# Layer 0 state space: B products of every third unit by ScalarE and TensorE, two thirds of the C products on GpSimd

## The chip, the cores and the metric

The kernel runs on one core of a Trainium2 chip. The metric is the device time in microseconds (us) of that core, the median of three runs. A core has TensorE (PE, with its weight load PEld), VectorE (DVE), ScalarE (ACT), GpSimd (POOL) and the queue of SyncE (SP), which issues most DMAs. Each engine takes its own instructions in order and waits for the others at semaphores. PSUM is written by TensorE and can be read and written by VectorE and ScalarE here; GpSimd's operands all lie in SBUF.

## The reference

The model has two layers, each a state-space block and a mixture of experts. The change is in the state space of layer 0, on 4 batches of 1024 tokens with 256 inner channels and 16 states. Cut to what matters:

```
x_dbl = xp @ Wx.T                       # 64 + 16 + 16 columns
dlt, B, C = split(x_dbl)
delta = softplus(dlt @ Wdt.T + bdt)
A = -exp(A_log)
# for each channel d and each state n, over the tokens t:
h[t] = exp(delta[t,d] * A[d,n]) * h[t-1] + delta[t,d] * xp[t,d] * B[t,n]
y[t,d] = sum_n C[t,n] * h[t] + xp[t,d] * Dp[d]
out = (y * silu(z)) @ Wo.T
```

The reference works in chunks of 16 tokens; the kernel computes the same recurrence by one scan along the tokens.

## The kernel before

Channels lie on the 128 partitions in two halves (j = 0, 1), tokens along the free axis. A **unit** g is one state n of one column half c (512 tokens) of one batch b: a batch has UNITS = 32 units, TOTAL is 128. Position s is g % 32; s 0 to 15 are column half 0, s 16 to 31 half 1. `u` is delta times xp. For each unit

- ScalarE makes the decay exp(delta A) for both halves, `state_decay` (L563), into one of DS = 5 PSUM banks `decay`. Its wait is for the scan or C product five half-units back. In column half 0 it first copies the last column of the bank's former content to `carry` (L560), for the units whose states end in that bank.
- GpSimd makes the B product `bu` = u times row B, broadcast to all partitions, both halves in one instruction of 128x1024 (`make_bu`, L687), LEAD = 3 units ahead of its step. The row comes by a DMA of 256 KB (`load_b`, L222) into one of BS = 4 buffers; `bu` has BUS = 5 buffers.
- VectorE scans each half: state = decay * state + bu (L780), in place in the bank, or, in the units `on_pool` (s % 3 == 2), into the SBUF buffer `h` (HS = 6 buffers).
- The C product, state times row C (`load_c`, L231, CS = 5 buffers), is made by VectorE for each half (L790), and for the units on_pool by GpSimd in one instruction in place in `h` (`times_c`, L697), after a copy of the last column to `carry` (L695) in column half 0.
- TensorE adds h to `y_ps` by an identity matmul of 512 columns for each half (`add_state`, L416), two instructions each in the trace, for unit s - 2 at its step s.

The order on each engine is written out by hand. Every engine runs the same loop over b and s: at step g GpSimd makes B of g + 3, then C of g - 1 where that unit is its own; ScalarE makes the decays of g + 1. Between them stands the next batch's preparation, `pieces(b, s)`: x (four projections of 4 taps each, L336), z, low, v (L381, L386), each one made by TensorE in the single bank `piece` and read by ScalarE one step later, which frees it. ScalarE also has two silus of 1024 columns twice, each pair with two loads of its tables (s 12 for z, s 14 for x), softplus at s 23 to 25 and, from batch 1 on, the normalised rows `hat` from s 25. `gate` (L796) on VectorE takes y_ps of a column half at s 18 (half 0) and at s 1 of the next batch (half 1). TensorE's `skip` (L406) starts the next half of y_ps after it, `project_out` (L433) makes the output rows at s 22 and s 2. VectorE's `make_delta` is L801. After the stage come routing, experts, a second state space and its experts; the change doesn't touch them.

## Time and profile before

| | us |
|---|---|
| median of 3 runs | 1180.13 (1178.96 to 1181.77) |
| span of the profiled execution | 1175.1 |
| stage of layer 0's state space in it, first scan to the gate after the last | 35.6 to 505.0 |

The time of the profiled execution as a whole isn't given apart from its span. The median of the runs lies 5.0 us above the span, which is what lies around the span; sums are made in the span and these 5.0 us are added. Times in the rows are from the span's start. A busy time overlaps a little with the next instruction's, so an engine's pace is its start to start.

### The profile page before, as it was taken

To read this page: it belongs to the slowest core of one execution; us is meant where nothing else is said; L and a number is where in the kernel's file an instruction comes from. 1 tells how busy PE (TensorE), PEld (TensorE's weight loads), DVE (VectorE), ACT (ScalarE), POOL (GpSimd) and SP (SyncE) were. 2 spreads that over 40 slices of the span, in tenths; PEclk is the share of its full clock that TensorE was granted. 3 is DMA by queue.
4 is the path that set the end of the run, shared out by engine and by line. 5 is a ranking of instruction groups with operands and counts; after the bars stand their busy time and mean duration, and the time that the engine had idled before them with its cause. 6 is when DMAs were issued, how large, how long until landed. Compare 5 with 4: busy or idle time off the path is not lost. (4 is left out here: it accounts for less than half of the span.)

```text
span 1175.1 us, 14982 instructions
## 1 busy us (share of the span) xinstructions
PE 878.0 (75%) x4244; PEld 565.5 (48%) x4244; DVE 887.3 (76%) x1790; ACT 630.2 (54%) x1401; POOL 738.3 (63%) x508
## 2 busy tenths in 40 slices
PE   7797769886987787753999736596987978349930
PEld 4243324334433433333999713264665767339920
DVE  4896999899979999966666555486896878465512
ACT  4787635874587465516343313656567684246710
POOL 0898799989988999702666376355433443037646
PEclk8999989998999898865999967598989977569975
DMA  6644445455544554340233312111101020142323
GB/s 185 184 131 131 125 147 166 137 157 160 162 131 143 164 164 156 113 164 13 71 85 87 72 50 68 45 34 50 45 2 64 28 74 19 54 165 73 71 63 98
DMA packets 90905, 118.95 MB, mean 101 GB/s; under 512 B 12508, under 2 KB 48804, under 8 KB 90696
## 3 DMA queue, kind: packets, MB, share of 16 engines
q1 hardware_dynamic: 84168, 104.34, 28.7%
q0 software_dynamic: 6656, 13.64, 5.0%
q8 instruction: 36, 0.59, 0.2%
q14 instruction: 45, 0.37, 0.1%
HBM read 103.70 MB, written 14.25 MB: 100 GB/s over the span
## 5 line engine op out<-in xcount | busy, mean ns | idle before, releaser
L687 POOL TENSOR_TENSOR ma_bu<-ma_u,ma_row_b 128x1024 f32<-128x1024 f32 x128 | 300.7, 2377 | 15.6 <-DVE ma_u L898 8.0
L416 PE MATMUL y_ps<-ma_h,ident 128*128 128x512 f32 x512 | 254.1, 635 | 27.4 <-POOL ma_h L697 23.1
L1215 POOL DMA_INDIRECT s_rows<-xs,take x112 | 128.9, 1151 | 162.3 <-POOLq L951 105.6
L563 ACT ACTIVATE decay_ps<-ma_delta,negA 128x512 f32<-128x512 f32 x256 | 172.5, 686 | 85.8 <-DVE ma_h L790 82.9
L416 PEld LDWEIGHTS y_ps<-ma_h,ident 128*128 128x128 f32 x512 | 100.4, 204 | 156.1 <-issue 111.1
L1568 POOL TENSOR_TENSOR mi_dec<-mi_dec,mi_gm 128x512 f32<-128x512 f32 x32 | 40.7, 1272 | 135.0 <-DVE mi_gm L2033 111.5
L1232 PE MATMUL s_up_ps<-s_xt,s_w 128*128 128x128 f32 x896 | 122.6, 282 | 1.2 <-ACT s_xt L1259 1.2
L780 DVE TENSOR_TENSOR_SCAN decay_ps<-decay_ps,ma_carry,ma_bu 128x512 f32<-128x512 f32 x88 | 110.1, 1271 | 12.6 <-issue 9.7
L790 DVE TENSOR_TENSOR ma_h<-decay_ps,ma_row_c 128x512 f32<-128x512 f32 x176 | 116.9, 665 | 0.0
L1232 PEld LDWEIGHTS s_up_ps<-s_xt,s_w 128*128 128x128 f32 x896 | 113.2, 198 | 1.6 <-DVE s_w L1291 1.0
L697 POOL TENSOR_TENSOR ma_h<-ma_h,ma_row_c 128x1024 f32<-128x1024 f32 x40 | 97.1, 2428 | 17.4 <-DVE ma_h L780 15.6
L780 DVE TENSOR_TENSOR_SCAN decay_ps<-decay_ps,ma_bu 128x512 f32<-128x512 f32 x88 | 104.2, 1204 | 2.5 <-POOL ma_bu L687 2.5
L1241 PE MATMUL s_out_ps<-s_w,s_ht 128*128 128x128 f32 x608 | 87.3, 278 | 6.3 <-DVE s_outs L1308 6.1
L1550 POOL DMA_INDIRECT mi_y<-ys,where x64 | 64.1, 1002 | 36.1 <-issue 17.2
L1241 PEld LDWEIGHTS s_out_ps<-s_w,s_ht 128*128 128x128 f32 x608 | 76.4, 191 | 9.0 <-DVE s_ht L1298 4.4
L1291 DVE COPY s_w<-w 128x768 f32 (+1 forms) x112 | 71.3, 641 | 5.9 <-DVE s_outs L1311 1.9
L1624 PE MATMUL mi_pre<-hT,wc 128*128 128x512 f32 x128 | 60.4, 617 | 1.7 <-ACT hT L1768 1.5
L1298 DVE TENSOR_TENSOR s_ht<-s_up_ps,s_act_g 128x256 f32<-128x256 f32 x72 | 30.4, 423 | 40.2 <-ACT s_act_g L1266 21.8
L1271 ACT ACTIVATE s_ht<-s_up_ps,s_w 128x128 f32<-128x128 f32 x160 | 45.8, 369 | 24.6 <-PE s_up_ps L1232 23.9
L780 DVE TENSOR_TENSOR_SCAN ma_h<-decay_ps,ma_bu 128x512 f32<-128x512 f32 x40 | 48.2, 1205 | 7.5 <-issue 6.1
L1259 ACT ACTIVATE s_xt<-s_xt_ps 128x128 f32<-128x128 f32 x112 | 31.8, 283 | 37.4 <-PE s_xt_ps L1224 34.6
L1266 ACT ACTIVATE s_act_g<-s_up_ps 128x256 f32<-128x256 f32 x72 | 27.7, 384 | 44.8 <-PE s_up_ps L1232 44.2
(323 smaller groups left out, 1766.0 us busy)
## 6 DMA issues: line engine op xcount, KB each, us to landing
ma_row_b<-bc_rows SPq DMA_DIRECT2D x128, 256.0 KB, 3.6
ma_row_c<-bc_rows SPq DMA_DIRECT2D x128, 256.0 KB, 3.3
mi_cs<-cs_rows SPq DMA_DIRECT2D x32, 256.0 KB
ys<-s_outs SPq DMA_DIRECT2D x28, 256.0 KB
...
```

What stands on the lines that cost most here:

```text
L416: mm = pe.matmul(y_ps[:, j, :], m.ident[:], h[g % HS][:, j, :], start=False, stop=True, skip_group_check=True)
L563: act.activation(decay[s % DS][:], delta[b % 2][:, j, col(c)], ACT.Exp, scale=m.negA0[:, j, n:n + 1]).then_inc(decay_done, 1)
L687: pool.tensor_tensor(bu[g % BUS][:], u[b % 2][:, :, col(c)], both(row_b[g % BS]), ALU.mult).then_inc(bu_done, 1)
L697: pool.tensor_tensor(hs[:], hs[:], both(row_c[g % CS]), ALU.mult).then_inc(pool_product_done, 1)
L780: dve.tensor_tensor_scan(dst, d[:], bu[g % BUS][:, j, :], past, ALU.mult, ALU.add).then_inc(scan_done, 1)
L790: dve.tensor_tensor(h[g % HS][:, j, :], decay[s % DS][:], row_c[g % CS][:], ALU.mult).then_inc(product_done, 1)
L1215: pool.indirect_dma_start(rows[s % ROWS][:], None, m.xs[layer], bass.IndirectOffsetOnAxis(ap=m.take[:, s:s + 1], axis=0)).then_inc(fetched ...
L1232: mm = pe.matmul(up_ps[s % 2][:, f * P:(f + 1) * P], w[s % WS][:, f * P:(f + 1) * P], xt[s % 2][:], start=True, stop=True)
L1241: mm = pe.matmul(out_ps[s % 2][:, 0:P], ht[s % HS][:, f * P:(f + 1) * P], w[s % WS][:, UP + f * P:UP + (f + 1) * P], start=(f == 0), stop= ...
L1291: dve.tensor_copy(w[s % WS][:], m.w[layer][:, bass.ds(expert, 1), :].rearrange("p o f -> p (o f)")).then_inc(copied, 1)
L1550: pool.indirect_dma_start(fetched_rows[G % FETCH][k][:, t, :], None, m.ys[0], bass.IndirectOffsetOnAxis(ap=m.where[:, k, T:T + 1], axis=0) ...
L1624: mm = pe.matmul(bank[:], weights, m.hT[:, n, c * COL + k:c * COL + k + COL], start=(k == taps[0]), stop=(k == taps[-1]))
```

## The change

Per batch the units now fall in three kinds: s % 3 == 0 as before (call them V: bu by GpSimd, C by VectorE), s % 3 == 2 as before (call them P: bu and C by GpSimd), and s % 3 == 1 from unit 4 on (`by_turning`, call them T). These are 43 of the 128 units, 10 in the first batch and 11 in each other. For a T unit

- `u` has been turned (tokens on the partitions) into `u_rows`, by TensorE transposes and a copy by ScalarE, four pieces a batch, and B into `b_rows`, two pieces a batch (96 rows turned).
- ScalarE multiplies turned u by B, which is now a value for each partition: four instructions of 128x256, SBUF to SBUF, with the scale from `b_rows` (`scale_rows`), at step g - 2.
- TensorE turns the product back, eight transposes of 128x128 into the two decay banks of that unit (`turn_input`), at the head of its step g - 1, ahead of that step's pieces and of `add_state`.
- The decay goes to the SBUF tile `turned_decay` (one buffer for each half) instead of a bank, and VectorE's scan reads it and the bank and writes `h`.
- The unit is on_pool: its C product and its carry copy are GpSimd's.

No DMA of row B is made for a T unit. BS goes from 4 to 3, BUS from 5 to 4, counted in units whose bu GpSimd makes. The last unit, 127, is a T unit.

```diff
-    BS, CS, BUS, HS, DS, XS = 4, 5, 5, 6, 5, 3
+    BS, CS, BUS, HS, DS, XS = 3, 5, 4, 6, 5, 3
-    on_pool = lambda g: g % UNITS % 3 == 2
+    by_turning = lambda g: g % UNITS % 3 == 1 and g >= 4
+    on_pool = lambda g: g % UNITS % 3 == 2 or by_turning(g)
+    U_ROWS, B_ROWS, FIRST_B_ROWS = ((29, 30), (9, 12)), (25, 26), 3
...
+            def turn_input(g):
+                pe.wait_ge(bu_rows_done, turned_input[g] + 1)
+                for j in range(HALVES):
...
+                    if on_pool(before):
+                        pe.wait_ge(scan_done, s - DS + 1)
...
+                    for t in range(HT):
+                        tr = pe.transpose(decay[s % DS][:, t * P:(t + 1) * P], bu_rows[:, t, j * P:(j + 1) * P], m.ident[:])
+                    tr.then_inc(bu_turned, 1)
...
                 for s in range(UNITS):
+                    if b * UNITS + s + 1 in turned_input:
+                        turn_input(b * UNITS + s + 1)
...
+            def scale_rows(g):
...
+                if k > 0:
+                    act.wait_ge(bu_turned, 2 * k)
+                for t in range(HT):
+                    ins = act.activation(bu_rows[:, t, :], u_rows[c][:, t, :], ACT.Identity,
+                                         scale=b_rows[b % 2][:, c * HT + t, 2 * n:2 * n + 1])
...
+                    if g + 2 in turned_input:
+                        scale_rows(g + 2)
...
-                if g + LEAD < TOTAL:
+                if g + LEAD in pool_input:
                     make_bu(g + LEAD)
                 if g > 0 and on_pool(g - 1):
                     times_c(g - 1)
...
+                if by_turning(g):
+                    dve.wait_ge(bu_turned, 2 * turned_input[g] + j + 1)
+                    kept, added = turned_decay[:, j, :], d[:]
+                else:
+                    dve.wait_ge(bu_done, pool_input[g] + 1)
+                    kept, added = d[:], bu[pool_input[g] % BUS][:, j, :]
```

GpSimd in column half 1 of the first batch, before:

```order
L687 TENSOR_TENSOR ma_bu<-ma_u,ma_row_b 128x1024 x3
L697 TENSOR_TENSOR ma_h<-ma_h,ma_row_c 128x1024
L687 TENSOR_TENSOR ma_bu<-ma_u,ma_row_b 128x1024 x2
L679 TENSOR_TENSOR ma_u<-ma_delta,ma_xp 128x2x512
L687 TENSOR_TENSOR ma_bu<-ma_u,ma_row_b 128x1024
```

and after, the same place:

```order
L768 TENSOR_TENSOR ma_bu<-ma_u,ma_row_b 128x1024
L778 TENSOR_TENSOR ma_h<-ma_h,ma_row_c 128x1024
L768 TENSOR_TENSOR ma_bu<-ma_u,ma_row_b 128x1024
L778 TENSOR_TENSOR ma_h<-ma_h,ma_row_c 128x1024
L760 TENSOR_TENSOR ma_u<-ma_delta,ma_xp 128x2x512
```

Three B products to one C product have become one to one; the number of products is the same.

TensorE at s 17 to 25 of the first batch, before (L416 add_state, L386 v, L406 skip, L433 project_out, L366 hat):

```order
L381 MATMUL piece_ps<-ma_xp,wx 96x512 x2
L416 MATMUL y_ps<-ma_h,ident 128x512 x2
L386 MATMUL piece_ps<-ma_low,wdt 128x512
L406 MATMUL y_ps<-ma_xp,diagD 128x512 x2
L416 MATMUL y_ps<-ma_h,ident 128x512 x2
L386 MATMUL piece_ps<-ma_low,wdt 128x512
L416 MATMUL y_ps<-ma_h,ident 128x512 x2
```

and after (L455 add_state, L471 turn_input, L411 v, L445 skip):

```order
L406 MATMUL piece_ps<-ma_xp,wx 96x512 x2
L455 MATMUL y_ps<-ma_h,ident 128x512 x2
L471 MATMUL decay_ps<-ident,ma_bu_rows 128x128 x8
L411 MATMUL piece_ps<-ma_low,wdt 128x512
L445 MATMUL y_ps<-ma_xp,diagD 128x512 x2
L455 MATMUL y_ps<-ma_h,ident 128x512 x2
L411 MATMUL piece_ps<-ma_low,wdt 128x512
```

The eight transposes stand in front of the step's piece and its add, and behind the add of the step before.

## Rows read from the trace of the kernel before

**Rows 1.** The page's first line.

```profile
span 1175.1 us, 14982 instructions
```

**Rows 2.** Busy time by stretch: us, engines, granted clock (1.00 is full), DMA share, GB/s.

```profile
33.00:151.00 118.00, 94.45 (x230) 38.69 (x229) 104.39 (x111) 84.12 (x149) 105.16 (x56) 0.96 0.46 139
151.00:266.60 115.60, 95.58 (x228) 41.04 (x228) 110.67 (x124) 72.93 (x126) 107.61 (x59) 0.92 0.49 150
266.60:382.20 115.60, 97.70 (x256) 44.88 (x256) 108.97 (x124) 74.94 (x130) 105.91 (x59) 0.93 0.48 151
382.20:502.00 119.80, 94.91 (x254) 45.24 (x255) 119.56 (x139) 64.58 (x117) 106.86 (x60) 0.88 0.46 147
sum 469.00, PE 382.64 PEld 169.84 DVE 443.59 ACT 296.56 POOL 425.53; mean PE 95.66 PEld 42.46 DVE 110.90 ACT 74.14 POOL 106.38
```

**Rows 3.** Timeline of VectorE near 200 us: start, duration, instruction.

```profile
199.46 0.67 DVE L790 TENSOR_TENSOR ma_h<-decay_ps,ma_row_c 128x512 f32<-128x512 f32 x1
200.05 1.21 DVE L780 TENSOR_TENSOR_SCAN decay_ps<-decay_ps,ma_bu 128x512 f32<-128x512 f32 x1
```

**Rows 4.** Groups on GpSimd from 30 to 502 us: count, busy, mean ns, idle before.

```profile
L687 POOL TENSOR_TENSOR ma_bu<-ma_u,ma_row_b 128x1024 f32<-128x1024 f32 x128 | 300.7, 2377 | 15.6 <-DVE ma_u L898 8.0 <-DVE decay_ps L780 7.4
L697 POOL TENSOR_TENSOR ma_h<-ma_h,ma_row_c 128x1024 f32<-128x1024 f32 x40 | 97.1, 2428 | 17.4 <-DVE ma_h L780 15.6
L695 POOL COPY ma_carry<-ma_h 128x2 f32<-128x2 f32 x20 | 4.2, 212 | 6.8 <-DVE ma_h L780 6.2
```

**Rows 5.** Who VectorE waited for, 30 to 502 us: total, times, longest.

```profile
DVE decay_ps L780 <- issue: 9.7, 2, 6.9
DVE ma_h L780 <- issue: 6.1, 3, 3.0
DVE ma_h L780 <- ACT decay_ps L563: 1.4, 1, 1.4
```

**Rows 6.** Last product of GpSimd, last scans, and the gate behind them (timeline).

```profile
494.89 2.35 POOL L697 TENSOR_TENSOR ma_h<-ma_h,ma_row_c 128x1024 f32<-128x1024 f32 x1 [5.19 <-DVE ma_h L780]
499.39 1.28 DVE L780 TENSOR_TENSOR_SCAN decay_ps<-decay_ps,ma_carry,ma_bu 128x512 f32<-128x512 f32 x1
499.58 5.40 PE L416 MATMUL y_ps<-ma_h,ident 128*128 128x512 f32 x12
505.01 1.22 DVE L796 TENSOR_TENSOR ma_sz<-y_ps,ma_sz 128x1024 f32<-128x1024 f32 x1 [3.17 <-PE y_ps L416]
```

**Rows 7.** VectorE's delta with GpSimd idle, then beside its B product (timeline).

```profile
257.48 1.21 DVE L801 TENSOR_TENSOR ma_delta<-ma_delta,ma_u 128x1024 f32<-128x1024 f32 x1
261.75 2.74 DVE L801 TENSOR_TENSOR ma_delta<-ma_delta,ma_u 128x1024 f32<-128x1024 f32 x1
```

**Rows 8.** Groups on ScalarE from 30 to 502 us, and a pair of hats (timeline).

```profile
L563 ACT ACTIVATE decay_ps<-ma_delta,negA 128x512 f32<-128x512 f32 x256 | 172.5, 686 | 85.8 <-DVE ma_h L790 82.9
L516 ACT ACTIVATE ma_sz<-piece_ps 128x512 f32<-128x512 f32 x16 | 9.4, 586 | 4.3 <-PE piece_ps L336 4.3
...
256.25 0.86 ACT L579 ACTIVATE ma_hat<-X,ma_shift,ma_var 128x128 f32<-128x128 f32 x2
```

**Rows 9.** TensorE: 18 matmuls of 512 columns, 4 transposes (timeline).

```profile
248.38 7.89 PE L416 MATMUL y_ps<-ma_h,ident 128*128 128x512 f32 x18
257.25 0.63 PE L366 MATMUL piece_ps<-ident,ma_hat 128*128 128x128 f32 x4
```

**Rows 10.** Busy time by stretch, columns as in rows 2.

```profile
210.00:225.00 15.00, 13.37 (x32) 5.48 (x30) 10.87 (x13) 14.69 (x25) 14.50 (x16) 1.00 0.45 149
```

**Rows 11.** The same, short stretches with TensorE busy and idle.

```profile
215.00:220.00 5.00, 5.00 (x13) 2.22 (x12) 4.71 (x6) 4.94 (x7) 4.58 (x7) 1.00 0.30 105
265.00:270.00 5.00, 1.08 (x5) 1.08 (x6) 5.00 (x7) 1.94 (x3) 5.00 (x3) 0.50 0.27 102
```

More of the change, by code:

```diff
@@ L106, in pieces @@
                 out += [("columns", 0, 0)]
+            if s == 0:
+                out += [("b_rows", 0, 0), ("u_rows", 0, 0), ("u_rows", 0, 1)]
+            if s == FIRST_B_ROWS:
+                out += [("b_rows", 0, 1)]
             if s == FIRST_LOW:
@@ L115, in pieces @@
             out += [("z", b, Z.index(s))]
+        if s in U_ROWS[1]:
+            out += [("u_rows", b, 2 + U_ROWS[1].index(s))]
         if b + 1 < NBATCH:
+            if s in B_ROWS:
+                out += [("b_rows", b + 1, B_ROWS.index(s))]
             if s in XP:
@@ L122, in pieces @@
                 out += [("v", b + 1, s - V)]
+            if s in U_ROWS[0]:
+                out += [("u_rows", b + 1, U_ROWS[0].index(s))]
         if b > 0 and s in TURN:
@@ L156, in mamba @@
         h = [sb(f"h{i}", [P, HALVES, COL]) for i in range(HS)]
+        turned_decay = sb("turned_decay", [P, HALVES, COL])
+        u_rows = [sb(f"u_rows{c}", [P, HT, D_IN]) for c in range(NCOL)]
+        bu_rows = sb("bu_rows", [P, HT, D_IN])
+        b_rows = [sb(f"b_rows{r}", [P, BT, 2 * N0]) for r in range(2)]
         carry = sb("carry", [P, HALVES, N0])
@@ L386, in make @@
                     mm = pe.matmul(bank, m.wdt0[:, j * P:(j + 1) * P], low[0:RANK, col(c)], start=True, stop=True)
+                elif kind == "u_rows":
+                    c = i // 2
+                    pe.wait_ge(u_done, 2 * b + c + 1)
+                    for q in range(2):
+                        t = c * HT + i % 2 * 2 + q
+                        for j in range(HALVES):
+                            mm = pe.transpose(bank[:, q * D_IN + j * P:q * D_IN + (j + 1) * P],
+                                              u[b % 2][:, j, t * P:(t + 1) * P], m.ident[:])
+                elif kind == "b_rows":
+                    pe.wait_ge(piece_read, read("low", b, i))
+                    for t in range(HT):
+                        mm = pe.transpose(bank[:, t * (RANK + 2 * N0):(t + 1) * (RANK + 2 * N0)],
+                                          low[:, i * COL + t * P:i * COL + (t + 1) * P],
+                                          m.ident[0:RANK + 2 * N0, 0:RANK + 2 * N0])
                 elif kind == "columns":
@@ L562, in state_decay @@
                         act.wait_ge(act_carry, act_kept[before] + side + 1)
-                act.activation(decay[s % DS][:], delta[b % 2][:, j, col(c)], ACT.Exp, scale=m.negA0[:, j, n:n + 1]
-                               ).then_inc(decay_done, 1)
+                dst = decay[s % DS][:]
+                if by_turning(g):
+                    dst = turned_decay[:, j, :]
+                    k = turned_input[g]
+                    if k > 0:
+                        act.wait_ge(scan_done, 2 * inputs_turned[k - 1] + j + 1)
+                act.activation(dst, delta[b % 2][:, j, col(c)], ACT.Exp, scale=m.negA0[:, j, n:n + 1]
+                               ).then_inc(decay_done, 1)
+            def scale_rows(g):
+                b, c, n = g // UNITS, half_of(g), g % N0
+                k = turned_input[g]
+                act.wait_ge(piece_read, max(read("u_rows", b, 2 * c + 1), read("b_rows", b, c)))
+                if k > 0:
+                    act.wait_ge(bu_turned, 2 * k)
+                for t in range(HT):
+                    ins = act.activation(bu_rows[:, t, :], u_rows[c][:, t, :], ACT.Identity,
+                                         scale=b_rows[b % 2][:, c * HT + t, 2 * n:2 * n + 1])
+                ins.then_inc(bu_rows_done, 1)
             def root(b):
```

54 lines of the change are left out of this document (38 added, 16 removed).

## The prediction

> **What bounds the kernel now.** I read the busy times by stretch first. From 33 to 502 us VectorE is busy 443.6 us of 469, GpSimd 425.5, TensorE 382.6, ScalarE 296.6 [rows 2]. So VectorE sets the pace: it has almost no idle time in the last stretch (119.56 of 119.80), and in the first (104.39 of 118.00) what holds it is in its list of waits. There "issue" and the decays, which are both ScalarE's work coming late behind silus, table loads and softplus, make up 9.7 + 6.1 + 1.4 = 17.2 us [rows 5]. GpSimd is right behind it, and TensorE isn't far. A change that takes work from VectorE is therefore worth what GpSimd has left, and GpSimd gets no relief here.
>
> The stage's end is a chain: GpSimd's last product ends at 494.89 + 2.35 = 497.24, VectorE's last scan at 499.39 + 1.28 = 500.67, TensorE adds three units up to 505, and the gate begins at 505.01 [rows 6]. What follows the gate is untouched, so a shift of the gate is a shift of the whole span.
>
> **VectorE.** 43 units lose two C products each. From a product's start to the next scan's pass 200.05 - 199.46 = 0.59 us [rows 3], so 86 x 0.59 = 50.7 us go, and 443.6 becomes about 393. The scan of a T unit still reads one operand in SBUF and one in PSUM, and writes SBUF as the P units' scans do; only the places of the two are exchanged. I cost that at nothing. Its cover is thin if I am wrong: 0.1 us for each of 86 scans is 8.6 us, VectorE would then stand at 401, still under GpSimd. VectorE with both operands in SBUF is what hurts: the same delta takes 1.21 us alone and 2.74 us beside GpSimd's product [rows 7]. The Trainium skill says that too (GPSIMD Engine Reference, Key points: GpSimd shares its SBUF interfaces with VectorE and collides with VectorE instructions of two SBUF inputs); by it the new scans, with one SBUF input, are safe, and the two rows agree.
>
> **GpSimd.** It drops 43 B products and takes 43 C products. Their means are 2377 and 2428 ns [rows 4]: the difference is between 0 (the means hold a few long ones beside VectorE's two-operand instructions) and 43 x 0.05 = 2.2 us. I take 0. It gains 19 carry copies of 0.212 us [rows 4], 4.0 us, with the wait behind each perhaps 5. Its work goes from 425.5 to 430.5 us and it is now the engine with most to do. From 33.0 to its last product's end it has 464.2 us, thus 38.7 us idle before, nearly all of it waits for scans [rows 4]. The gain is how much of these 38.7 us goes.
>
> **ScalarE.** Per T unit four instructions of 128x256 with a scale for each partition. No row has this form. From below: two hats of 128 columns with bias and scale take 0.86, 0.43 each; from above: the decay's 512 columns take 0.686 [rows 8]. I take 0.47, near the hat, because a column costs little beside the fixed part. 172 x 0.47 = 81 us (74 to 118). The copies into u_rows, 16 x 0.586 [rows 8] = 9.4, and into b_rows, 8 x about 0.3 = 2.4; less 38 carry copies of some 0.2 each = -7.6. ScalarE goes from 296.6 to about 382 of some 450 us, 85%. By sum it isn't the bound. By place it is: in the stretch 210 to 225 it was already busy 14.69 of 15 us and VectorE fell to 10.87, so 4.1 us were lost to it there, while GpSimd, with its B products made ahead, stayed at 14.50 [rows 10]. One more `scale_rows` (1.9 us) and a u_rows copy fall into each such stretch. I let VectorE's holds grow from 17.2 to 29 us, three us in each of four batches.
>
> How much of that reaches GpSimd? VectorE can be ahead of GpSimd's C products by the 3 units of LEAD, but the T unit's input comes from TensorE behind the adds of earlier C products, which leaves it one and a half units, about 5 us. A hold of 4 to 7 us is half hidden: 14 us.
>
> **TensorE.** 18 matmuls of 512 columns take 7.89 us, 0.43 each; four transposes begin and end within 0.63 [rows 9], and of that about 0.2 is the last one's way through the array, so I take 0.11 each at full clock (0.16 from above). Per batch the code issues 192 instructions of 512 columns (128 adds, 32 x, 8 each z, low, v, skip) = 82 us, and output, hats and logits about 10. New: 88 transposes into the banks, 16 of u, 8 of low: 112 x 0.11 = 12.3 (17.9 from above). Sum 104, against GpSimd's 108 to 109 a batch (105.9 to 107.6 [rows 2] and the copies). Not the bound on average, but unevenly spread: from s 4 to 15 (12 units) TensorE has 20.5 of adds, 17.1 of x and z, 1.7 of skip, 1.8 of u_rows and row pieces and 3.6 of T inputs = 44.7 us where GpSimd has 12 x 3.4 = 41; from s 16 to 23 it has about 29 against 27. So it falls 5 us behind in each batch that prepares another, and catches up after s 24. `turn_input` stands in that queue, behind the add of the step before, which waits for GpSimd; the T scan waits for it, and the decays five half-units on wait for the scan. Half of 5 us in three batches reaches GpSimd: 7 us.
>
> **DMA and SP.** 43 row loads of 256 KB go. In SP's queue each remaining load_b stands at least four GpSimd products before its use, so the smaller BS and BUS cost nothing; a load's landing would have to take over 9 us to show.
>
> **The end.** Unit 127 is now GpSimd's: after the last scan come 2.35 us of C product and four matmuls (1.7), 4.1 us to the gate, against 505.01 - 500.67 = 4.3 before [rows 6]. Equal. But the last four C products have no B products between them, so GpSimd waits there for scans, 4 us.
>
> **The sum.** GpSimd's end: 33.0 + 430.5 of work + 14 (ScalarE) + 7 (TensorE) + 4 (end) = 488.5. The last scan is 2.35 before that, 486.1; it was 500.67. The gate and the span come 14.5 us earlier: 1175.1 [rows 1] - 14.5 = 1160.6, and 5.0 for what lies around the span: 1165.6, say 1165.5.
>
> **The rivals.**
>
> A. *The engines locked together, no change.* ScalarE's new instructions cost 0.6 rather than 0.47 (+22 us), and the holds reach GpSimd almost whole because VectorE never gets ahead: 25 (ScalarE) + 11 (TensorE) + 4 (end) = 40 us idle rather than 25. Then the last scan ends at 33 + 430.5 + 40 - 2.35 = 501.2, where it ended before: 1180.6, from 1176 to 1185. For it: GpSimd at 89% and more in every stretch [rows 2] leaves little room. Against: ScalarE's waits for VectorE are 82.9 us [rows 8], so it has time to catch up.
>
> B. *TensorE becomes the bound, slower.* The place is `turn_input` in TensorE's in-order queue. The granted clock is 0.50 (1.2 GHz) in a stretch where TensorE is busy 1.08 us of 5, and 1.00 (2.4 GHz) where it is busy throughout [rows 11], and the granted mean is 0.88 to 0.96 [rows 2]. If transposes cost 0.3 each rather than 0.11, a batch has 104 + 112 x 0.19 = 125 us of TensorE against 115.6 now, +9.7 in each of the two middle batches, and with a first batch unchanged the time is 1180 + 19 = 1199; at 0.2 each it is 114, which with the uneven spread gives 119 and +7, 1187. The point from which it decides is about 0.18 us a transpose. Against it stands 0.63 for four [rows 9]. The Trainium skill has a rule on that side (TensorE: Matmul & The Clock Gate, Part 4: PE-mode transpose): about 275 ns for a transpose in a kernel's context, and transposes don't raise the clock. By that figure, as an estimate, it would be near 1195; the row of four in 0.63 speaks against its first half, and no row here separates the second.
>
> C. *More than forecast.* ScalarE's holds are swallowed by the lead and GpSimd runs at 97%: idle 12 rather than 25, 13 us more: 1152.
>
> D. *The change doesn't relieve VectorE*, because T scans cost 0.3 us more each with the operands exchanged: 26 us, VectorE at 419 with 29 of holds, 448; gain about 8 at most: 1172 to 1178.
>
> **How the numbers follow.** Forecast 1165.5 with what lies near it (1157 to 1174) 50%; C 12%; A 15%; B 13%; D 10%. A measurement of this kernel tells about 0.2% (2.4 us) from no change. Faster: forecast, C, a third of A, most of D: 74% less a margin for what I don't see, 70%. Same: 10%. Slower: B and the rest of A, 20%. The range leaves out half of C and the far part of B: 1152 to 1187.
>
> **What would show it.** GpSimd's busy share in the stage at 94% or more with its waits for scans under 25 us; VectorE's busy time near 393 and its waits near 60 us, now for B products and for transposes; T scans of 1.20 and 1.27 us; ScalarE's four at 0.4 to 0.5 each; TensorE's transposes 0.11 apart; the gate near 490. It is wrong if the scans' longest wait is for TensorE's turned inputs (B), if GpSimd idles over 35 us (A), or if the T scans are longer than the others (D).

## The result and the profile after

| | before | changed |
|---|---|---|
| median, us | 1180.95 (1178.96 to 1181.94, 4 runs) | 1209.35 (1206.58 to 1212.92, 4 runs) |
| last gate of layer 0's state space, us | 505.0 | 537.5 |
| span of the profiled execution, us | 1175.1 | 1211.1 |

The changed kernel is slower: its time is 1.0237 of the kernel before, interval 1.0206 to 1.0269. The prediction said 1165.5 us and faster, range 1152 to 1187. The profiled execution itself took 1212.92 us. The gate moved by 32.5 us and the span by 36.0; what follows the gate varies between 663 and 676 us from one profiled execution to the next, so below the kernels are compared by the time of that gate. Each gate is from one execution. The first scan starts between 34.9 and 36.6 us in these traces, and a part of a batch that two kernels share can differ too: batch 0's s 0 to 3 takes 24.3 us in the changed kernel and 21.8 in one below (g3) that doesn't alter it. A difference of 3 us or less between two gates therefore says nothing.

Busy time by stretch, columns as in [rows 2]; the last stretch is new, since the stage now lasts until 537:

```profile
span 1211.1 us, 16060 instructions
```

```profile
33.00:151.00 118.00, 100.43 (x297) 46.91 (x296) 78.79 (x82) 89.55 (x168) 87.52 (x53) 0.90 0.34 103
151.00:266.60 115.60, 100.25 (x296) 47.65 (x294) 89.74 (x94) 77.99 (x145) 99.92 (x61) 0.91 0.38 117
266.60:382.20 115.60, 101.39 (x351) 52.77 (x352) 88.84 (x94) 86.18 (x160) 100.72 (x61) 0.96 0.36 115
382.20:502.00 119.80, 101.89 (x353) 52.58 (x352) 105.21 (x110) 88.36 (x170) 113.50 (x66) 0.94 0.43 129
502.00:540.00 38.00, 33.44 (x133) 18.80 (x132) 30.43 (x34) 21.21 (x41) 28.28 (x13) 0.96 0.30 87
sum 507.00, PE 437.40 PEld 218.72 DVE 393.01 ACT 363.30 POOL 429.95; mean PE 87.48 PEld 43.74 DVE 78.60 ACT 72.66 POOL 85.99
```

VectorE is busy 393.0 us and GpSimd 430.0, the amounts forecast (393 and 430.5). Neither is near the 507 us of these stretches. Against [rows 2], GpSimd fell from 105.2 to 87.5 us in the first stretch and from 107.6 to 99.9 in the next: its work was put off, not taken away.

The groups of the stage, columns as in [rows 4] (L866 is the scan, L768 and L778 GpSimd's products, L641 the scaled copies, L471 `turn_input`):

```profile
L866 DVE TENSOR_TENSOR_SCAN ma_h<-ma_turned_decay,ma_carry,decay_ps 128x512 f32<-128x512 f32 x48 | 61.0, 1270 | 39.1 <-issue 29.3 <-PE decay_ps L471 9.8
L866 DVE TENSOR_TENSOR_SCAN ma_h<-ma_turned_decay,decay_ps 128x512 f32<-128x512 f32 x38 | 46.1, 1214 | 37.1 <-PE decay_ps L471 37.1
L768 POOL TENSOR_TENSOR ma_bu<-ma_u,ma_row_b 128x1024 f32<-128x1024 f32 x85 | 203.2, 2394 | 15.1 <-DVE ma_u L984 8.0 <-DMA ma_row_b<-bc_rows 6.9
L778 POOL TENSOR_TENSOR ma_h<-ma_h,ma_row_c 128x1024 f32<-128x1024 f32 x83 | 198.5, 2394 | 27.9 <-DVE ma_h L866 24.8
L641 ACT ACTIVATE ma_bu_rows<-ma_u_rows,ma_b_rows 128x256 f32<-128x256 f32 x172 | 72.8, 496 | 0.0
L471 PE MATMUL decay_ps<-ident,ma_bu_rows 128*128 128x128 f32 x344 | 44.6, 273 | 0.0
```

And for whom VectorE waited, columns as in [rows 5]:

```profile
DVE ma_h L866 <- PE decay_ps L471: 46.9, 22, 7.9
DVE ma_h L866 <- issue: 35.9, 8, 10.3
DVE ma_sz L882 <- PE y_ps L455: 22.4, 8, 6.2
```

The scans of T units are hardly longer than others, but 46.9 us of idle time stand before them for TensorE's turned input and 29.3 under "issue" (35.9 with the other scans into `h`). The holds of VectorE, 17.2 us in [rows 5], have become 82.8.

**Where the time lies.** The starts of the scans give the time of each part of a batch. Sums over the four batches, us:

| | s 0-3 | s 4-11 | s 12-15 | s 16-31 | last gate |
|---|---|---|---|---|---|
| before | 57.0 | 107.2 | 67.0 | 233.8 | 505.0 |
| changed | 74.2 | 103.7 | 92.6 | 224.5 | 537.5 |

So column half 1 gained 9.3 us and s 4 to 11 gained 3.5, while s 12 to 15, where the silus stand, lost 25.6 and s 0 to 3 lost 17.2, 10.3 of them in the first batch alone. The first scan starts 0.7 us later, and from the last scan's end to the gate it takes 1.9 us more. The last batch, which prepares no other, took 103.2 us against 104.5. That is all the exchange brought there; GpSimd is busy 96.3 us of these 103.2.

Busy time in batch 1, columns as in [rows 2]: s 4 to 11 and s 12 to 15 of the kernel before,

```profile
181.09:206.32 25.23, 25.23 (x60) 11.16 (x59) 25.23 (x32) 15.30 (x33) 24.84 (x13) 1.00 0.57 175
206.32:222.53 16.21, 16.21 (x39) 7.08 (x38) 12.08 (x15) 15.47 (x22) 15.63 (x17) 1.00 0.45 136
```

and s 0 to 3, 4 to 11, 12 to 15, 16 to 23 and 24 to 31 of the changed one:

```profile
177.54:195.02 17.48, 13.80 (x50) 7.10 (x49) 12.61 (x15) 8.76 (x18) 17.13 (x10) 0.90 0.42 137
195.02:221.59 26.57, 26.57 (x81) 13.04 (x80) 21.81 (x26) 16.23 (x33) 22.57 (x15) 1.00 0.43 136
221.59:247.40 25.81, 22.41 (x62) 10.61 (x61) 10.98 (x12) 19.56 (x30) 16.64 (x18) 0.87 0.27 82
247.40:274.87 27.47, 24.93 (x75) 11.21 (x75) 23.70 (x23) 21.98 (x44) 23.82 (x12) 0.94 0.37 120
274.87:304.15 29.28, 22.54 (x90) 12.15 (x89) 27.70 (x30) 23.80 (x45) 29.28 (x12) 0.94 0.33 107
```

This is the row that the prediction lacked. From s 4 to 15 of this batch of the kernel before TensorE was busy for all of 25.23 + 16.21 us at full clock, beside GpSimd with 40.5 of 41.4. There was next to no room on TensorE there, and nothing for GpSimd to gain. Batch 2 is alike; in batch 0 TensorE was idle 6.7 us of 52.3. The change puts more on TensorE in just that place.

**In the x stretch without silus** (batch 2, timeline as in [rows 3]) TensorE has no gap; three units take 341.22 - 330.05 = 11.17 us from one `turn_input` to the next, and the T scan waits for it:

```profile
330.05 1.04 PE L471 MATMUL decay_ps<-ident,ma_bu_rows 128*128 128x128 f32 x8
330.68 1.22 DVE L866 TENSOR_TENSOR_SCAN ma_h<-ma_turned_decay,decay_ps 128x512 f32<-128x512 f32 x1 [1.96 <-PE decay_ps L471]
330.92 1.02 PE L361 MATMUL piece_ps<-hT,wz 128*128 128x512 f32 x2
331.78 1.88 PE L455 MATMUL y_ps<-ma_h,ident 128*128 128x512 f32 x4
333.50 3.60 PE L361 MATMUL piece_ps<-hT,wc 128*128 128x512 f32 x8
336.93 1.88 PE L455 MATMUL y_ps<-ma_h,ident 128*128 128x512 f32 x4
...
341.22 1.04 PE L471 MATMUL decay_ps<-ident,ma_bu_rows 128*128 128x128 f32 x8
```

**In the silu stretch** (batch 1) the delays form a chain through the one bank `piece` and the in-order queues:

```profile
226.54 1.28 ACT L740 ACT_TABLE_LOAD   x1
227.27 1.22 DVE L866 TENSOR_TENSOR_SCAN ma_h<-ma_turned_decay,decay_ps 128x512 f32<-128x512 f32 x1 [2.78 <-PE decay_ps L471]
227.50 0.60 PE L418 MATMUL piece_ps<-ident,ma_u 128*128 128x128 f32 x4
227.84 2.00 ACT L740 ACTIVATE ma_sz<-ma_sz 128x1024 f32<-128x1024 f32 x2
...
232.59 0.58 ACT L588 ACTIVATE ma_u_rows<-piece_ps 128x512 f32<-128x512 f32 x1
...
233.22 6.42 PE L361 MATMUL piece_ps<-hT,wc 128*128 128x512 f32 x8 [3.40 <-ACT ma_u_rows L588]
...
239.68 0.69 ACT L568 ACTIVATE ma_xp<-piece_ps,cb 128x512 f32<-128x512 f32 x1 [5.12 <-PE piece_ps L361]
240.27 1.69 ACT L641 ACTIVATE ma_bu_rows<-ma_u_rows,ma_b_rows 128x256 f32<-128x256 f32 x4
241.98 1.28 ACT L734 ACT_TABLE_LOAD   x1
...
246.59 0.72 ACT L631 ACTIVATE ma_turned_decay<-ma_delta,negA 128x512 f32<-128x512 f32 x1
...
247.40 1.28 DVE L866 TENSOR_TENSOR_SCAN ma_h<-ma_turned_decay,ma_carry,decay_ps 128x512 f32<-128x512 f32 x1 [10.32 <-issue]
```

The turned piece of u (227.50) lies in the bank while ScalarE makes the silus of z, with two table loads, and two decays; its copy comes at 232.59, and TensorE has waited 3.40 us for the bank. The x piece behind it takes 6.42 us where it took 3.60 in the stretch above; the granted clock is 0.50 (1.2 GHz) in the 2.70 us after that pause and 0.61 in the next 3.50 (columns as in [rows 2]):

```profile
233.30:236.00 2.70, 2.70 (x4) 1.15 (x5) 2.70 (x3) 1.26 (x2) 2.28 (x7) 0.50 0.52 179
236.00:239.50 3.50, 3.50 (x7) 1.47 (x6) 1.08 (x2) 0.00 (x0) 3.42 (x3) 0.61 0.03 12
```

ScalarE, in order, waits 5.12 us for this piece with the scaled copies, the silus of x and two table loads queued behind it, and the next decay comes at 246.59. VectorE is idle 10.32 us for it. In batch 1 the four units s 12 to 15 take 25.81 us instead of 16.21, GpSimd busy 16.64 of them.

**The start** of batch 0, TensorE and the first T scan (unit 4):

```profile
44.95 1.12 PE L418 MATMUL piece_ps<-ident,ma_u 128*128 128x128 f32 x4 [4.83 <-ACT ma_b_rows L591]
46.75 1.11 PE L418 MATMUL piece_ps<-ident,ma_u 128*128 128x128 f32 x4 [0.69 <-ACT ma_u_rows L588]
48.55 3.73 PE L406 MATMUL piece_ps<-ma_xp,wx 128*96 128x512 f32 x4 [0.69 <-ACT ma_u_rows L588]
...
60.58 1.22 DVE L866 TENSOR_TENSOR_SCAN ma_h<-ma_turned_decay,decay_ps 128x512 f32<-128x512 f32 x1 [7.95 <-PE decay_ps L471]
```

The pieces that turn B and u go through TensorE and ScalarE one by one (four matmuls of low in 3.73 us at a granted clock of 0.50; the same four take 1.88 at 245.51); low, v, the skip and the first adds stand behind them, and `turn_input` behind all. Unit 4 starts at 60.6 instead of 49.6.

**The end** answers to [rows 6]:

```profile
531.41 2.35 POOL L778 TENSOR_TENSOR ma_h<-ma_h,ma_row_c 128x1024 f32<-128x1024 f32 x1 [3.48 <-DVE ma_h L866]
532.06 5.40 PE L455 MATMUL y_ps<-ma_h,ident 128*128 128x512 f32 x12
537.50 1.23 DVE L882 TENSOR_TENSOR ma_sz<-y_ps,ma_sz 128x1024 f32<-128x1024 f32 x1 [6.23 <-PE y_ps L455]
```

### The profile page after: what moved, and what is told of

Its sections match the earlier page's. It is cut to its first block and busy times, and to the rows that moved or that the text cites. A ratio compares the mean times of both kernels' runs of the same rounds, so it can differ in the third digit from the quotient of the medians.

```text
span 1211.1 us, 16060 instructions
## 1 busy us (share of the span) xinstructions
PE 930.8 (77%) x4684; PEld 614.5 (51%) x4684; DVE 834.7 (69%) x1704; ACT 696.3 (57%) x1559; POOL 745.2 (62%) x527
## 5 line engine op out<-in xcount | busy, mean ns | idle before, releaser
L455 PE MATMUL y_ps<-ma_h,ident 128*128 128x512 f32 x512 | 256.9, 632 | 16.6 <-POOL ma_h L778 16.6
L778 POOL TENSOR_TENSOR ma_h<-ma_h,ma_row_c 128x1024 f32<-128x1024 f32 x83 | 198.5, 2394 | 27.9 <-DVE ma_h L866 24.8
L768 POOL TENSOR_TENSOR ma_bu<-ma_u,ma_row_b 128x1024 f32<-128x1024 f32 x85 | 203.2, 2394 | 15.1 <-DVE ma_u L984 8.0
L455 PEld LDWEIGHTS y_ps<-ma_h,ident 128*128 128x128 f32 x512 | 97.5, 202 | 130.0 <-issue 99.4
L631 ACT ACTIVATE decay_ps<-ma_delta,negA 128x512 f32<-128x512 f32 x170 | 113.3, 683 | 28.0 <-DVE ma_h L876 25.2
L1637 POOL DMA_INDIRECT mi_y<-ys,where x64 | 65.5, 1024 | 36.6 <-issue 17.1
L866 DVE TENSOR_TENSOR_SCAN ma_h<-ma_turned_decay,ma_carry,decay_ps 128x512 f32<-128x512 f32 x48 | 61.0, 1270 | 39.1 <-issue 29.3
L641 ACT ACTIVATE ma_bu_rows<-ma_u_rows,ma_b_rows 128x256 f32<-128x256 f32 x172 | 72.8, 496 | 0.0
L866 DVE TENSOR_TENSOR_SCAN ma_h<-ma_turned_decay,decay_ps 128x512 f32<-128x512 f32 x38 | 46.1, 1214 | 37.1 <-PE decay_ps L471 37.1
L866 DVE TENSOR_TENSOR_SCAN decay_ps<-decay_ps,ma_bu 128x512 f32<-128x512 f32 x50 | 58.2, 1208 | 6.2 <-ACT decay_ps L631 3.7
L631 ACT ACTIVATE ma_turned_decay<-ma_delta,negA 128x512 f32<-128x512 f32 x86 | 58.1, 710 | 5.9 <-DVE ma_h L866 5.9
L876 DVE TENSOR_TENSOR ma_h<-decay_ps,ma_row_c 128x512 f32<-128x512 f32 x90 | 60.1, 668 | 0.0
L1358 ACT ACTIVATE s_ht<-s_up_ps,s_w 128x128 f32<-128x128 f32 x160 | 45.8, 370 | 24.6 <-PE s_up_ps L1319 24.5
L1385 DVE TENSOR_TENSOR s_ht<-s_up_ps,s_act_g 128x256 f32<-128x256 f32 x72 | 30.5, 423 | 40.5 <-ACT s_act_g L1353 22.9
```

Of the source, the lines that this page charges most:

```text
L455: mm = pe.matmul(y_ps[:, j, :], m.ident[:], h[g % HS][:, j, :], start=False, stop=True, skip_group_check=True)
L631: act.activation(dst, delta[b % 2][:, j, col(c)], ACT.Exp, scale=m.negA0[:, j, n:n + 1]).then_inc(decay_done, 1)
L641: ins = act.activation(bu_rows[:, t, :], u_rows[c][:, t, :], ACT.Identity, scale=b_rows[b % 2][:, c * HT + t, 2 * n:2 * n + 1])
L768: pool.tensor_tensor(bu[k % BUS][:], u[b % 2][:, :, col(c)], both(row_b[k % BS]), ALU.mult).then_inc(bu_done, 1)
L778: pool.tensor_tensor(hs[:], hs[:], both(row_c[g % CS]), ALU.mult).then_inc(pool_product_done, 1)
L866: dve.tensor_tensor_scan(dst, kept, added, past, ALU.mult, ALU.add).then_inc(scan_done, 1)
```

## The experiments

**First question: which of the new costs is it?** Six versions of the changed kernel, each with one cost made smaller, moved or given back.

e1_no_t_in_burst makes units 13 and 16 of each batch as before the change:

```
-    by_turning = lambda g: g % UNITS % 3 == 1 and g >= 4
+    by_turning = lambda g: g % UNITS % 3 == 1 and g >= 4 and g % UNITS not in (13, 16)
```

> The changed kernel, but units s 13 and 16 of each batch are made as before (B product by GpSimd, C product by VectorE): no T unit where ScalarE has its silus and table loads. Theory (the turned input hangs in ScalarE's and TensorE's queues behind the silus of s 12 to 16): s 12 to 16 goes back from 92.6 us over the four batches to 70 to 75, the time falls from 1209 by 15 to 22 us, to about 1190. Rival (TensorE's work: 2 of 11 T units fewer takes a fifth of the loss): 1203 to 1205.

e2_c_on_vector gives the C products of the T units back to VectorE:

```
-    on_pool = lambda g: g % UNITS % 3 == 2 or by_turning(g)
+    on_pool = lambda g: g % UNITS % 3 == 2
```

> Half of the change alone: inputs of T units are turned as in the changed kernel, but their C products stay on VectorE, in the bank, so GpSimd loses 43 products and VectorE none. Theory (the queue behind the silus, not who makes C): the loss at s 12 to 16 stays, VectorE's 50 us come back elsewhere; 1210 to 1225. Rival (the C products on GpSimd hold TensorE's adds and so the turned inputs): faster than the changed kernel, 1185 to 1200.

e3_quarter_scale makes one of the four scaled copies of a T unit (behind the first such unit), e4_quarter_turn one of four transposes:

```
-                for t in range(HT):                                # scale_rows
+                for t in range(HT if k == 0 else 1):
```

```
-                    for t in range(HT):                            # turn_input
+                    for t in range(HT if turned_input[g] == 0 else 1):
```

> Leaves out three of the four scaled copies of each T unit after the first one (the tile keeps old values), which takes some 54 us from ScalarE and nothing else. Theory (place in the queue, bursts of silus): only some 1.3 us in each of the two burst stretches of a batch and a little at s 0 to 4, 6 to 12 us: 1198 to 1203. Rival (ScalarE's added work as such): 20 us or more, under 1190.

> Leaves out three of each four transposes back into the banks after the first T unit, 28 us of TensorE at full clock. Theory: helps at s 4 to 12 only, where TensorE is busy without a gap (0.65 us in each three units), 4 to 9 us: 1200 to 1205. Rival (TensorE's added work, at half clock or not, is the bound all along): 20 us or more, under 1190.

e5_scale_first lets ScalarE make its scaled copies ahead of reading the step's piece (and turns the first half of u at s 28 and 29, one step earlier); e6_u_rows_early turns the second half of u at s 3 and 9 instead of 9 and 12, away from the silus, from batch 1 on (TensorE's wait for the former batch's output moves from s 4 to s 3 with it):

```
+                    if g + 2 in turned_input:
+                        scale_rows(g + 2)
...
-                    if g + 2 in turned_input:
-                        scale_rows(g + 2)
```

```
-        if s in U_ROWS[1]:
-            out += [("u_rows", b, 2 + U_ROWS[1].index(s))]
+        late = U_ROWS[1] if b == 0 else (3, 9)
+        if s in late:
+            out += [("u_rows", b, 2 + late.index(s))]
```

> ScalarE makes a T unit's scaled copies before it reads that step's pieces instead of behind them (and the pieces of turned u for column half 0 stand one step earlier). Theory (the T input waits in ScalarE's queue behind the read of an x piece that TensorE hasn't made yet): at s 12 to 16 and s 4 to 12 the turned input is there earlier; the silus themselves stay: 5 to 15 us, 1195 to 1204. Rival (work, not place): within 3 us of 1209.

> From the second batch on the turned u of column half 1 comes at s 3 and 9 instead of 9 and 12, so that no extra piece stands in the single piece bank at the silus of s 12. Theory (TensorE waits 3.4 us for ScalarE to free the bank, drops to half clock and takes 6.4 us for the x piece instead of 3.6, and ScalarE waits 5.1 us for that): in two batches some 5 to 7 us each at s 12 to 16, 1196 to 1201. Rival (the bank's piece is only one of many delays): within 4 us of 1209.

Measured, with the ratio to the kernel before (us; parts of a batch summed over four). The kernel before had medians between 1174.8 and 1182.6 us beside these and the later runs, so the ratio and not the median compares with it:

| | median | ratio (95%) | s 0-3 | s 4-11 | s 12-15 | s 16-31 | gate |
|---|---|---|---|---|---|---|---|
| changed | 1209.35 | 1.0237 (1.0206-1.0269) | 74.2 | 103.7 | 92.6 | 224.5 | 537.5 |
| e1 | 1206.94 | 1.0198 (1.0145-1.0250) | 74.9 | 103.7 | 85.3 | 227.7 | 532.4 |
| e2 | 1231.41 | 1.0413 (1.0359-1.0466) | 71.3 | 111.1 | 89.0 | 244.4 | 556.5 |
| e3 | 1197.38 | 1.0121 (1.0082-1.0160) | 72.4 | 103.3 | 84.7 | 221.4 | 523.6 |
| e4 | 1198.04 | 1.0120 (1.0072-1.0169) | 71.3 | 100.8 | 89.7 | 223.5 | 527.2 |
| e5 | 1207.08 | 1.0275 (1.0191-1.0360) | 73.9 | 103.3 | 83.0 | 234.3 | 537.0 |
| e6 | 1194.43 | 1.0185 (1.0119-1.0250) | 74.3 | 104.6 | 82.6 | 226.0 | 529.3 |

No single cost is the loss. Without three quarters of ScalarE's copies the gate is 13.9 us earlier, without three quarters of the transposes 10.3, and both stay slower than the kernel before. e1, without the T units of the silu stretch, was expected to bring s 12 to 15 to 70 to 75 us; it is 85.3, and the gate is 5.1 us earlier. e2 shows that the relief of VectorE was real: given back, it costs 19.0 us more, and more than was expected. e5 mended s 12 to 15 by 9.6 us and lost all of it between s 16 and 31, as its rival said. e6 takes 8.2 us off by moving the two turned pieces of u: that is the link through the bank at 227.50 above. In batches 1 and 2, where they are moved, s 12 to 15 falls from 25.8 and 24.6 us to 20.1 each (before: 16.2 and 17.9).

e4 also shows what TensorE's time is worth from s 4 to 11. There the six transposes of eight that it leaves out are 0.65 us of a T unit, and the stretch of batch 1, with two such inputs in it, goes from 26.57 to 25.26 us: each microsecond on TensorE counts whole. But s 12 to 15 of that batch still takes 24.5.

**Second question: are the silus the cause?** e7_after_no_silu and e8_before_no_silu take the work of the silus of x and z, and their table loads, out of the changed kernel and of the kernel before (one column each stays, for the order). The edit for x is shown, that for z is alike. What is left of the difference isn't due to them.

```
-                            act.activation(xs[:], xs[:], ACT.Silu).then_inc(silu_done, 1)
-                        act.preload_act_table_set("natural_log_exp_and_others")
+                            act.activation(xs[:, 0, 0:1], xs[:, 0, 0:1], ACT.Copy).then_inc(silu_done, 1)
```

> The changed kernel without the silus of z and of x inside the loop and their table loads (one column is copied instead), so that ScalarE has no bursts. To be set against the kernel before cut in the same way. Theory (bursts): the gap between the two, 28 us with silus, shrinks to 5 or less, or turns. Rival (work on ScalarE or TensorE all along): the gap stays over 20 us.

> The kernel before without the same silus and table loads: 4 to 12 us faster than with them by what VectorE waits for ScalarE there (17.2 us in all, some of it at softplus): 1168 to 1177. The gap to the changed kernel cut in the same way is the measure.

| | median | ratio (95%) | s 0-3 | s 4-11 | s 12-15 | s 16-31 | gate |
|---|---|---|---|---|---|---|---|
| e7 | 1178.01 | 1.0019 (0.9988-1.0049) | 72.1 | 103.7 | 64.0 | 224.8 | 507.2 |
| e8 | 1159.20 | 0.9871 (0.9802-0.9941) | 57.0 | 107.6 | 47.6 | 234.3 | 487.0 |

The difference of the gates is still 20.2 us, so the silus make 12.3 of the 32.5 and the view that the bursts alone are the loss falls (5 us or less was expected to remain). The ratios say the same: they are 0.0148 apart, some 17 us, where it was 28. Even without them s 12 to 15 is 16.4 us longer than in e8. In batch 1 of e7, s 4 to 11, 12 to 15 and 16 to 23 (columns as in [rows 2]):

```profile
182.06:208.64 26.58, 26.58 (x81) 13.05 (x80) 21.80 (x26) 16.24 (x33) 22.54 (x15) 1.00 0.44 136
208.64:224.21 15.57, 15.57 (x51) 7.80 (x50) 10.88 (x12) 11.46 (x28) 14.04 (x16) 1.00 0.39 120
224.21:251.06 26.85, 26.85 (x87) 12.56 (x86) 23.71 (x24) 21.46 (x42) 26.29 (x15) 1.00 0.47 133
```

TensorE is busy without a gap for 69 us, at full clock, while ScalarE and VectorE have time to spare. The kernel before without silus (e8) takes 25.23 and 11.91 us for the first two stretches, also with TensorE always busy; the changed one takes 5.0 us longer for them. That named the next suspect.

**Third question: is it TensorE's load?** g3_after_one_tap and g4_before_one_tap leave three of the four taps of the x projection out for batches 1 to 3, in the changed kernel and in the kernel before: 72 matmuls of 0.43, 31 us of TensorE in the places where x is made (s 4 to 15 of batches 0 to 2). That is more than the change put there: by the forecast's count 5.4 us a batch, 16 us in these three, an estimate. Silus, scaled copies and transposes stay.

```
-                    mm = project(bank, lambda k: m.wc0[:, k, j * P:(j + 1) * P], b, c, range(TAPS))
+                    mm = project(bank, lambda k: m.wc0[:, k, j * P:(j + 1) * P], b, c, range(TAPS) if b == 0 else [PAD])
```

> The changed kernel with one tap instead of four in the x projections of batches 1 to 3, which takes 12 x 2.57 = 31 us of TensorE out of s 4 to 16 and nothing from the other engines. To be set against the kernel before cut alike. Theory M (TensorE's load in the x stretch is the loss): s 4 to 16, 196.4 us over the four batches with the change and 174.2 before, falls below 180 and the difference below 6; the gap of the last gates, 32.5, to about 15. Rival K (the in-order chain through ScalarE's silus and the piece bank, whatever TensorE's load): the difference stays over 15.

> The kernel before with one tap in the x projections of batches 1 to 3. GpSimd was busy 170 of the 174 us of s 4 to 16, so TensorE's relief should bring at most 4 us there: gate 501 to 505, time within 0.4% of before.

| | median | ratio (95%) | s 0-3 | s 4-11 | s 12-15 | s 16-31 | gate |
|---|---|---|---|---|---|---|---|
| g3 | 1185.67 | 1.0030 (1.0000-1.0060) | 71.5 | 90.2 | 78.9 | 223.8 | 506.5 |
| g4 | 1176.94 | 0.9964 (0.9933-0.9994) | 57.0 | 107.8 | 60.9 | 233.9 | 500.4 |

The difference of the gates falls from 32.5 to 6.1 us, that of the ratios to 0.0066, some 8 us. The kernel before gains 4.6 us from the same relief, the changed one 31.0. From s 4 to 15 the sums are now equal, 169.1 against 168.7, where they were 196.3 against 174.2. But that is a gain and a loss that meet: s 4 to 11 takes 17.6 us less than in g4, and s 12 to 15 still 18.0 more, in batch 0 alone 27.7 against 18.8. In batch 1 of g3, s 4 to 11 and s 12 to 15:

```profile
188.09:209.69 21.60, 20.95 (x67) 10.39 (x66) 21.60 (x25) 17.96 (x38) 19.51 (x13) 1.00 0.48 133
209.69:228.50 18.81, 16.22 (x49) 7.86 (x48) 10.99 (x13) 17.86 (x27) 18.07 (x20) 0.91 0.43 139
```

With TensorE relieved, the eight units take 21.60 instead of 25.23 us, VectorE busy throughout: the gain that the prediction meant is there. At s 12 to 15 they take 18.81 us, where the changed kernel takes 25.81, with all silus in place; g4 takes 15.0. So TensorE's load decides between gain and loss at s 4 to 11 and makes a part of the loss at s 12 to 15. The chain shown above needs all its links: of the 9.6 us that batch 1 loses at s 12 to 15, 3.7 are left without silus (e7 against e8), 3.8 with TensorE relieved (g3 against g4) and 3.9 with the turned u moved (e6). Each takes some 6 us away, so these are the same microseconds; what is left under each no run took away.

**Fourth question: can the place save it?** If s 4 to 15 and the start are the loss and column half 1 the gain, T units at s 19 and later should be faster than before. f3_first_later has no T unit before unit 19 of batch 0; f4_light has six a batch (s 1, 19, 22, 25, 28, 31; s 1 from batch 1 on), f1_light_only four (s 19, 22, 25, 28); f2_light_mixed is f1 with two of the four C products on VectorE.

```
f3:  by_turning = lambda g: g % UNITS % 3 == 1 and g >= 19
f4:  by_turning = lambda g: g % UNITS in (1, 19, 22, 25, 28, 31) and g >= 19
f1:  by_turning = lambda g: g % UNITS in (19, 22, 25, 28)
f2:  as f1, and on_pool = lambda g: g % UNITS % 3 == 2 or g % UNITS in (19, 25)
all:
-            if s == 0:
-                out += [("b_rows", 0, 0), ("u_rows", 0, 0), ("u_rows", 0, 1)]
f1, f2, f4: the second half of u turned as in e6;
f1, f2: no turned pieces for column half 0 at all
```

> The changed kernel without T units, turned u and turned B in column half 0 of the first batch. Theory (the pieces at s 0 and the T input of unit 4 hold the start by 10 us, the x stretch of that batch some 5 more): gate 519 to 525 instead of 537.5, time near 1195. Rival (the late start is taken up again later): gate over 530.

> T units at s 1, 19, 22, 25, 28 and 31, none in the x stretch and none in the first column half of the first batch. Theory: the x stretch is as before, s 0 to 4 keeps some 7 us of loss over three batches because the gate of the former half waits for unit 31's product on GpSimd; gate at 499 to 507, 3 to 8 us later than without 1 and 31. Rival (T units cost by their number): gate at 515 or later.

> T units only at s 19, 22, 25 and 28, where TensorE has no x pieces; the turned u and B rows of column half 0 are not made at all, the turned u of half 1 comes at s 3 and 9 from the second batch on. Theory (place: the loss is made in the stretch of x pieces, s 4 to 16, where TensorE is busy without a gap, at the silus, and at s 0 to 4; a gain exists at s 16 to 32 alone): s 0 to 16 takes what it took before, s 16 to 32 some 7 us less in all; the last gate at 494 to 501 instead of 505 before and 537.5 with the change, time 0.3 to 0.9% under before. Rival (a T unit costs wherever it stands): gate after 508.

> As the kernel with T units at s 19, 22, 25 and 28 only, but the C products of 22 and 28 stay on VectorE, so GpSimd has two products fewer in a batch and VectorE four short ones more. If GpSimd bounds that stretch: gate 1 to 3 us earlier than with all four C products on GpSimd. If VectorE bounds it: 1 to 4 us later.

| | median | ratio (95%) | s 0-3 | s 4-11 | s 12-15 | s 16-31 | gate |
|---|---|---|---|---|---|---|---|
| f3 | 1188.49 | 1.0115 (1.0054-1.0176) | 62.2 | 106.6 | 85.6 | 224.2 | 521.5 |
| f4 | 1179.12 | 1.0036 (1.0005-1.0068) | 62.2 | 107.7 | 71.7 | 225.3 | 507.7 |
| f1 | 1185.96 | 1.0089 (1.0057-1.0122) | 71.4 | 107.6 | 71.7 | 224.0 | 516.9 |
| f2 | 1181.67 | 1.0033 (1.0000-1.0066) | 57.8 | 107.7 | 73.3 | 230.3 | 508.5 |

f3 gets the start back: 12.0 us at s 0 to 3 (batch 0 takes 14.0 there, as before) and 7.0 at s 12 to 15, 16.0 in all. f4 gets nearly everything back and no gain. f1, which was to be the best at 494 to 501, is not: column half 1 gains 9.8 us and s 0 to 3 loses 14.4. In f1, f2 and f4 s 4 to 11 takes what it took before, though BS and BUS are smaller there too: the smaller buffers cost nothing in that place. The waits of VectorE in f1 show where (columns as in [rows 5]):

```profile
DVE ma_sz L879 <- PE y_ps L452: 25.8, 8, 7.0
DVE decay_ps L863 <- issue: 14.6, 3, 9.0
```

L879 is the gate. VectorE, relieved, had run ahead of GpSimd's C products through column half 1; the gate at s 1 of the next batch needs the last of them, and there it waited 14.1 us over the batches (4.5, 2.6 and 7.0). GpSimd started seven products at s 0 to 3 of these batches, where the order gives it five. f2, with two C products a batch less on GpSimd, waits there 0.5 us, and its gate is 8.4 us earlier. That f4 has fewer such waits than f1, with two T units more, was not expected and stays unexplained.

**Fifth question: does relief of VectorE alone help?** g1_two_more_c and g2_one_more_c are the kernel before, with two or one more C product a batch on GpSimd and nothing turned.

```
-    on_pool = lambda g: g % UNITS % 3 == 2
+    on_pool = lambda g: g % UNITS % 3 == 2 or g % UNITS in (19, 25)        # g1
+    on_pool = lambda g: g % UNITS % 3 == 2 or g % UNITS == 22              # g2
```

> The kernel before, without any turning, but GpSimd also makes the C products of units s 19 and 25: 4.7 us more of GpSimd in each batch where it idled 31.7 us over four batches (s 16 to 32), 4.7 us less of VectorE. Theory (there GpSimd has room for it and VectorE is the bound): s 16 to 32 up to 3 us less per batch, gate 495 to 503, unless the gate at s 1 takes it back. Rival (VectorE only runs ahead of GpSimd and waits at the next gate): gate 505 to 512.

> The same with one more C product on GpSimd, of unit s 22: half the effect. Theory: gate 500 to 504. Rival: 505 or later.

| | median | ratio (95%) | s 0-3 | s 4-11 | s 12-15 | s 16-31 | gate |
|---|---|---|---|---|---|---|---|
| g1 | 1184.04 | 1.0020 (0.9992-1.0047) | 64.6 | 107.2 | 65.4 | 227.2 | 509.4 |
| g2 | 1182.28 | 0.9996 (0.9970-1.0021) | 58.7 | 107.6 | 66.7 | 231.7 | 504.6 |

g1 gains 6.6 us from s 16 to 31 and pays 7.6 at s 0 to 3, the same giving back at the gate as in f1. It pays again at the last gate, which waits 7.57 us instead of 3.17 [rows 6]. Nothing is turned here, so this is the relief of VectorE alone. g2 changes nothing beyond the noise. No version here beat the kernel before.

## Why the prediction was wrong

The sizes of the work were right or nearly so; the idle time was not, because it was summed over the whole stage. The forecast for GpSimd's last end was 33.0 + 430.5 of work + 25 of idle time (14 ScalarE, 7 TensorE, 4 end). Measured it is 33.0 + 430.0 + 70.8 = 533.8. By place, GpSimd's idle time until the end of its last product, us:

| | to the first scan | s 0-3 | s 4-15 | s 16-31 | sum |
|---|---|---|---|---|---|
| before | 0.2 | 6.0 | 4.2 | 28.3 | 38.7 |
| changed | 0.9 | 9.4 | 38.6 | 21.9 | 70.8 |

- **VectorE**: forecast 393 us busy, measured 393.0. T scans take 1.214 and 1.270 us, those of P units, which write the same place, 1.202 and 1.258: exchanging the SBUF and the PSUM operand costs 1 us over 86 scans, and rival D falls.
- **GpSimd**: forecast 430.5, measured 430.0. The step that failed is the next one, "the gain is how much of these 38.7 us goes". They were taken as one sum, and all of them were let go. Only column half 1 had much to give, and it gave 6.4 us (9.3 of the stage's time), while s 4 to 15, which had 4.2, took 34.4 more. Of the 9.3 us some 6.9 came back at s 0 to 3 of the following batches (17.2 less the 10.3 of the start). In batch 1 GpSimd is busy 29.28 of 29.28 us at s 24 to 31 and 17.13 of 17.48 at s 0 to 3: behind, with the gate waiting (22.4 us in all above, 6.4 of them at s 1). f1 and g1 show this taking back without T units in column half 0, g1 without any. Part of it lies in the order: at s 0 to 3 it now gives GpSimd six products instead of five (C of units 31, 1 and 2, B of 3, 5 and 6), of 2.4 us each, and one fewer in column half 1. The prediction had no term for either.
- **ScalarE**: forecast 0.47 us a scaled copy, measured 0.40 from start to start, four in 1.69; forecast total 382, measured 363. The holds of VectorE were to grow from 17 to 29 us; they became 82.8, 46.9 of them for the turned input and 35.9 under "issue". The step that failed is that they were priced from ScalarE's own work (a scaled copy and a u_rows copy more). ScalarE waited for TensorE instead: 5.12 us in front of one x piece, half of the 10.32 us hold. e6 and e3 each shrink it, and with TensorE relieved (g3) s 12 to 15 is 13.7 us shorter with every copy still in place (6.1 in the kernel before).
- **TensorE**: forecast 0.11 us a transpose. Eight take 1.04 from begin to end, of which 0.27 is one transpose's own duration, so 0.11 each. The need from s 4 to 15 was put at 44.7 us, which is close to what the stretch takes when TensorE has no gap (e7: 26.58 + 15.57 = 42.2 in batch 1). What failed is what it was held against: GpSimd's 41 us, and "half of 5 us in three batches reaches GpSimd: 7 us". The stretch took 41.44 us before the change with TensorE busy for all of it, so there an added microsecond counts whole (e4), and late pieces hold ScalarE and through it everything else: in batch 1 the stretch grew by 10.9 us for some 5.4 of added work. The terms of ScalarE and TensorE, 14 + 7 us of idle time, are 38.6 us of GpSimd's idle time from s 4 to 15, and the stretch takes 22.1 us longer (196.3 - 174.2); it is 0.4 once TensorE has 31 us less to do.
- **The independent sum**: 14 for ScalarE and 7 for TensorE were added as if apart. At s 12 to 15 they are one loop: silus, late reading of the bank, TensorE's pause and lower clock, late x, ScalarE waiting in order, late decays. Without silus 20.2 of the 32.5 us remain, with TensorE relieved 6.1; the two together would take off 38.7, more than there is, so they overlap, or TensorE's relief gives more than its load took.
- **The start**: it has no term at all in the prediction. It costs 10.3 us in the first batch, and f3 takes it back.
- **DMA and SP**: forecast nothing. One wait of GpSimd for row B (6.9 us, before the first T scan) shows, within the late start. Without turned pieces at the start (f3, with the same buffers) s 0 to 3 takes 14.0 us as before, so the wait belongs to the late start and not to the smaller buffers as such.
- **The end**: equal was forecast; from the last scan's end to the gate it takes 6.2 us instead of 4.3. Of the 5.0 us that were put down to what lies around the span, only some 1.8 do: the changed kernel's profiled execution took 1212.92 us with a span of 1211.1. The rest was the distance of one execution from the median, 3 us in a forecast that was off by 44.
- **The rivals**: B named the right place, `turn_input` in TensorE's in-order queue, and the right sign, but hung it on a transpose of 0.18 us or more. At 0.11 it should not have come; it came because the room was already next to nothing in that stretch. The Trainium skill gives about 275 ns for a transpose in context (TensorE: Matmul & The Clock Gate, Part 4: PE-mode transpose); the trace agrees for the duration of one (273 ns on the mean of 344), and not for the pace, 0.11 us, by which a sum has to go. The page's other half, that transposes don't raise the clock, is not separated here: the stretch s 4 to 11 has them and a granted clock of 1.00, beside matmuls. A foresaw 40 us of idle GpSimd with no change in time; it has 70.8. C, less idle time than forecast, didn't come.

What stays open: how the 26 us of the gap that TensorE's relief removes divide between plain lack of room and the lower clock after its pauses. No run held the clock fixed. Nor was a second `piece` bank tried, which would cut the chain at the bank, nor `turn_input` one step earlier, which would show how much of the 46.9 us is its place in the queue. Batch 0 takes 27.9 us at s 12 to 15 instead of 20.8. TensorE's relief leaves 27.7 (g3), and without silus it is still 18.4 against 11.9 (e7, e8); what holds it there was not followed.
